# A fused attention and FFN block: the causal mask leaves the matrix engine, and the gate and up products are dealt over other beats

## The reference

```python
x = L0_attn_x                              # (4, 512, 512)
xn = _layernorm(x, axis=-1)
s = _L0_attn_ref(xn, w_qkv, w_out, q_gamma, k_gamma)
g = _silu(_L0_ffn_ref(xn, wq_gate, s_gate, wq_up, s_up, wq_down, s_down))
x = x + s * g

# attention: 16 heads of 32, per-head rmsnorm of q and k, rope, causal
mask = (q_idx >= k_idx) & (q_idx - k_idx <= WINDOW)      # WINDOW 1024 > 512
scores = einsum('bhqd,bhkd->bhqk', q, k) / sqrt(HD)
attn = softmax(where(mask, scores, NEG))
out = einsum('bhqk,bhkd->bhqd', attn, v) ... @ w_out

# ffn: W = (wq - 128) * scale, hidden size 1408
qlinear(silu(qlinear(x, wq_gate)) * qlinear(x, wq_up), wq_down)
```

## Time and profile before

| what | value |
|---|---|
| median of 3 runs | 791.72 us (791.6 to 792.12) |
| time of the profiled execution | 793.75 us |
| its span | 791.8 us |
| PE, PE weight load busy | 716.0 us, 575.5 us |
| DVE, ACT, POOL busy | 530.2, 450.1, 293.0 us |
| granted PE clock, mean of the span | 0.963 |

### The profile page before, as it was taken

One profiled execution on the slowest core, in us unless ns is written; L12 is line 12 of the kernel. 1 busy time (PEld: TensorE's weight loads), 2 busy tenths in 40 slices (PEclk: granted clock), 3 DMA queues, 4 the chain that ended last, 5 costly groups with the idle time before them and its releaser, 6 DMA issues.

```text
span 791.8 us, 12942 instructions
## 1 busy us (share of the span) xinstructions
PE 716.0 (90%) x4160; PEld 575.5 (73%) x4160; DVE 530.2 (67%) x1051; ACT 450.1 (57%) x1007; POOL 293.0 (37%) x338
## 2 busy tenths in 40 slices
PE   2589999989999999899999999999999944898997
PEld 2568887777787887777878777788887733676885
DVE  2677778887767676877666778777645673546373
ACT  1445666677666556776665567756555754534230
POOL 5443335555343344554443536544434310100000
PEclk9699999999999999999999999999999985699999
DMA  8154443412232332133333331233322163288672
GB/s 280 42 174 149 146 134 119 136 54 80 89 113 89 115 107 80 42 90 91 111 94 100 107 95 34 50 99 107 100 87 78 55 206 128 84 262 293 199 252 94
DMA packets 59281, 94.38 MB, mean 119 GB/s; under 512 B 12752, under 2 KB 15440, under 8 KB 59216
## 3 DMA queue, kind: packets, MB, share of 16 engines
q1 hardware_dynamic: 59216, 93.56, 37.4%
HBM read 59.06 MB, written 25.82 MB: 107 GB/s over the span
## 4 chain that ended last, share of the span: by engine, by line
PE 68%; DMA 7%; issue 7%; DVE 6%; POOL 6%; SPq 4%; ACT 2%; DVEq 0%; POOLq 0%; ACTq 0%
PE bank L1124 18%; PE bank L1019 14%; PE bank L1060 7%; PE bank L1140 6%; PE bank L1100 6%; PE bank L1081 5%; PE bank L1044 4%; PE bank L1031 3%; POOL rr L517 2%; PE bank L1046 2%; DMA rd_dram<-rd 2%; PE bank L1083 2%; POOL rb L526 2%; DMA rdb<-rd_dram 1%; SPq L346 1%
## 5 line engine op out<-in xcount | busy, mean ns | idle before, releaser
L517 POOL TENSOR_TENSOR rr<-ss,half 128x8 f32<-128x8 f32 x64 | 106.1, 1658 | 161.8 <-DVE ss L791 161.8
L842 DVE TENSOR_REDUCE mx<-bank 128x1 f32<-128x384 f32 (+3 forms) x176 | 109.6, 637 | 83.9 <-PE bank L1083 83.1
L625 ACT ACTIVATE pf<-bank 128x512 f32<-128x512 f32 (+1 forms) x192 | 100.7, 525 | 103.7 <-PE bank L1046 69.7
L823 DVE TENSOR_TENSOR pl<-pf,ph 128x512 fp32r<-128x512 f32 (+1 forms) x192 | 124.6, 649 | 19.0 <-ACT ph L626 18.8
L1124 PE MATMUL bank<-xnt_h,wgu 128*128 128x512 f32 x352 | 98.7, 402 | 4.6 <-DVE g L869 2.0
L523 POOL TENSOR_TENSOR ra<-qn,cg 128x256 f32<-128x256 f32 x64 | 58.2, 909 | 118.5 <-DVE qn L803 118.5
L626 ACT ACTIVATE ph<-bank 128x512 fp32r<-128x512 f32 (+1 forms) x192 | 100.9, 525 | 0.0
L1044 PE MATMUL bank<-qst,kst 97*128 97x512 f32 (+3 forms) x256 | 83.0, 377 | 16.1 <-DMA qst<-mrow 16.1
L1124 PE MATMUL bank<-xnt_l,wgu 128*128 128x512 f32 x352 | 96.3, 395 | 0.0
L1081 PE MATMUL bank<-kst,qst 96*128 96x128 f32 (+3 forms) x256 | 83.5, 377 | 1.3 <-DVE mx L842 1.3
L1060 PE MATMUL bank<-ph,va 128*65 128x512 f32 (+3 forms) x256 | 77.7, 328 | 5.0 <-ACT oraw L634 3.1
(11 more groups left out here) (84 smaller groups left out, 1406.8 us busy)
## 6 DMA issues: line engine op xcount, KB each, us to landing
wgu<-wg_dram SPq DMA_DIRECT2D x66, 256.0 KB, 2.8
hf_dram<-g SPq DMA_DIRECT2D x44, 256.0 KB, 3.2
hf_raw<-hf_dram SPq DMA_DIRECT2D x44, 256.0 KB, 5.8
wg_dram<-wgu SPq DMA_DIRECT2D x22, 256.0 KB, 3.1
xr<-x SPq DMA_DIRECT2D x16, 256.0 KB, 3.6
stage<-w_gu SPq DMA_DIRECT2D x16, 256.0 KB, 3.3
oh<-oraw SPq DMA_DIRECT2D x64, 64.0 KB, 2.0
ol<-oraw SPq DMA_DIRECT2D x64, 64.0 KB, 2.0
```

The lines of the kernel that those rows point to most:

```text
L517: pool.tensor_tensor(rr[:, s, :], ss[:, s, :], half[:], ALU.pow).then_inc(rr_ok, 1)
L625: act.activation(pf[:, tile], bank[:, 0:w], ACT.Exp, scale=SCALE)
L823: dve.tensor_tensor(pl[:, tile], pf[:, tile], ph[:, tile].bitcast(F32), ALU.subtract).then_inc(pl_ok, 1)
L842: dve.tensor_reduce(mx[:].rearrange("p (h t) -> p h t", t=TB)[:, h0:h0 + len(heads), qb], bank[:, 0:len(heads) * w].rearrange("p (h n) -> ...
```

## The change

- **No mask matmuls.** `scores_t` and `maxima` issue the score matmuls alone. For the maxima DVE now runs one `tensor_tensor_reduce` per head (it adds `msk_w`, a bf16 mask of 512 columns that is zero but for its last 128, writes the sum back to the bank and gives the maximum); in the compiled kernel each is an ISA instruction and a second one that writes the 128 x 1 result. There are 256 pairs in place of 160 reductions over scores. For the probabilities POOL zeroes what lies above the diagonal by `affine_select` on the high and low part together (`keep_past`, 128 x 2 x 128, 4 per head, 256 in all), and `p_v` waits for it (`tri_ok`). `norm` moves from k = 2 to k = 3.
- **Two beats of transposes.** The 4 row blocks of the next batch are transposed two by two in the places 9 and 10; the second of a beat goes through the bank of the gate products.
- **Gate and up products** of the batches 1 to 3 are dealt over 14 beats, from place 11 on: 1, then eight times 2 (places 12 to 3), then 1 in the places 4 to 8. Batch 0: two in each of the beats -3 to 6, one in 7 and 8.

```diff
-FIRST, PER_BEAT = -3, (2, 2, 2, 2, 2, 2, 2, 2, 1, 2, 1, 2)
+FIRST = (-3, -5, -5, -5)
+PER_BEAT = ((2, 2, 2, 2, 2, 2, 2, 2, 2, 2, 1, 1),) + ((1, 2, 2, 2, 2, 2, 2, 2, 2, 1, 1, 1, 1, 1),) * 3
...
+        def xt_at(c):
+            if c < 0:
+                return [(0, c + 7)] if 0 <= c + 7 < TB else []
+            b, k = c // 16 + 1, c % 16 - 9
+            return [(b, 2 * k), (b, 2 * k + 1)] if k in (0, 1) and b < B else []
+        def xt_bank(b, t):
+            return GU_PS if b and t % 2 else W_PS
...
+            def keep_past(j, e):
+                pool.wait_ge(pl_ok, NOP * j + e + 1)
+                for _, c0, _ in ST_OPS[e]:
+                    a = ST_AT[e] + c0
+                    op = pool.affine_select(pp[:, :, a:a + P], pp[:, :, a:a + P], [[0, 2], [1, P]], ALU.is_ge, 0.0,
+                                            base=0, channel_multiplier=-1)
+                op.then_inc(tri_ok, 1)
...
                 if there(j + 6, NB):
                     inv_rms(j + 6, (c + 6) % 2)
+                if there(j, NB):
+                    keep_past(j, 0)
                 if there(j + 6, NB):
                     rope(j + 6, (c + 6) % 2, (c + 6) % 4)
+                if there(j, NB):
+                    keep_past(j, 1)
...
-                if k == 2 and there(4 * r + (c - 6) // 4, B * G):
-                    norm(4 * r + (c - 6) // 4)
+                if k == 3 and there(4 * r + (c - 7) // 4, B * G):
+                    norm(4 * r + (c - 7) // 4)
+                if there(j, NB):
+                    keep_past(j, 2)
...
-                    dve.tensor_reduce(mx[...][:, h0:h0 + len(heads), qb],
-                                      bank[...], AX.X, ALU.max).then_inc(sm_ok, 1)
+                    for a, h in enumerate(heads):
+                        col = h * TB + qb
+                        op = dve.tensor_tensor_reduce(
+                            bank[:, a * w:(a + 1) * w], bank[:, a * w:(a + 1) * w], msk_w[:, N - w:N], 1.0, -3.0e38,
+                            ALU.add, ALU.max, mx[:, col:col + 1])
+                    op.then_inc(sm_ok, 1)
...
-                    pe.matmul(bank[:, c0:c0 + w], kst[...], qst[...], start=True, stop=False)
-                    op = pe.matmul(bank[:, c0:c0 + P], idb[:], msk_t[:], start=False, stop=True)
+                    op = pe.matmul(bank[:, c0:c0 + w], kst[...], qst[...], start=True, stop=True)
...
-                pe.wait_ge(pl_ok, NOP * j_ + e + 1)
+                pe.wait_ge(tri_ok, NOP * j_ + e + 1)
```

More of the change, by code:

```diff
@@ L222, in halves @@
         def halves(c):
[L224 to L228, removed]
+            for b in range(B):
+                rel = c - 16 * b - FIRST[b]
+                if 0 <= rel < len(PER_BEAT[b]):
+                    first = HALVES * b + sum(PER_BEAT[b][:rel])
+                    return list(range(first, first + PER_BEAT[b][rel]))
+            return []
         def half_at(c, index):
@@ L692, in o_out, with xn_out @@
                         o_evac(j - 1, 4 * r + (c - 1) // 4, (c - 1) % 4)
-                def xn_out():
-                    d, t = at(c, 9)
-                    if t is not None and there(r + 1 + d, B):
-                        xt_high(r + 1 + d, t)
+                def xn_out(index):
+                    for b, t in xt_at(c)[index:index + 1]:
+                        xt_high(b, t)
                 if turned:
                     t_high(j + 5, (c + 5) % 2)
-                xn_out()
+                xn_out(0)
                 gate(half_at(c - 1, 1))
@@ L903, in beat @@
                 gated(half_at(c - 1, 1))
-                d, t = at(c, 9)
-                if k != 3 and t is not None and there(r + 1 + d, B):
-                    xt_low(r + 1 + d, t)
+                if k != 3:
+                    for b, t in xt_at(c)[:1]:
+                        xt_low(b, t)
                 if mxs:
                     maxima(r, c + 4, SM_A[k])
-                if k == 3 and t is not None and there(r + 1 + d, B):
-                    xt_low(r + 1 + d, t)
+                if k == 3:
+                    for b, t in xt_at(c):
+                        xt_low(b, t)
                 if rms and k == 3:
@@ L1161, in turn_q @@
                             pe.wait_ge(s_ev, 4 * (r + d_o) + t_o + 1)
-                        if t_x is not None and there(r + 1 + d_x, B):
-                            pe.wait_ge(xt_lo, 4 * (r + 1 + d_x) + t_x + 1)
+                        for b, t in xts[:1]:
+                            pe.wait_ge(xt_lo, 4 * b + t + 1)
                         turn(r, c + 5, 0)
@@ L1176, in w_bank @@
                         out_proj(r + d_o, t_o, part)
-                    if part == 0 and early and t_x is not None and there(r + 1 + d_x, B):
-                        xn_turn(j + 4, r + 1 + d_x, t_x)
+                    if part == 0 and early:
+                        for b, t in xts:
+                            xn_turn(j + 4, b, t)
                 def w_free():
@@ L1190, in beat @@
                     scores_t(r, c, 0)
-                if not early and t_x is not None and there(r + 1 + d_x, B):
+                if not early and xts:
                     w_free()
-                    xn_turn(j + 4, r + 1 + d_x, t_x)
+                    for b, t in xts:
+                        xn_turn(j + 4, b, t)
                 if attend:
@@ L1212, in beat @@
                 turn_q()
-                if t_o is None and t_x is None:
+                if t_o is None and not xts:
                     banks(SM_B)
```

66 lines of the change are left out of this document (33 added, 33 removed).

## The result

The changed kernel takes 749.24 us (median of 4, 747.23 to 753.24) against 791.92 (median of 4 beside it): the ratio is 0.9465, 95% interval 0.9425 to 0.9506. The profiled execution took 753.24 us, the slowest of the four and 4.0 above their median, with a span of 751.2.

The account below looks back on a forecast made before the run. PE was taken to bound the middle, the `qn` loop the light beats. Savings of 6.5, 9.5, 9.5, 11.5, 1.0 and 1.5 us made 39.5: 754.3 for the profiled execution, 752 us against the median, range 740 to 760.

Parts of the forecast that it names:

- The likeliest case: Whole kernel: the forecast itself, a time of 740 to 760 us, chance 0.46.
- the `qn` loop: QKV bank's way from ACT to DVE, POOL and back to DVE, 7 to 8 us; the second limit, holding places 8 to 11.
- DVE's 90%: Sign against the forecast: DVE busy over 90% of a beat.
- The PE term: PE's work a batch: 128 masks at 0.125 us go, 16.0 us less, from 153.16 to 137.2.
- The stall terms: PE stalls a batch: 0.4 us in each of 12 full beats, 4.8, and 5.0 idle in the light beats.
- The DVE term: Masked reductions on DVE: 0.6 us a beat on top of 7.1, so 7.7 against PE's 8.6.
- The POOL term: Four selections a beat on POOL at 0.6 us each: from 4.5 to 6.9 us a beat.
- the second rival: DVE or POOL binds mildly, as selections slow DVE operations with two SBUF inputs: 760 to 782 us, chance 0.26.
- Beats 48 to 56: Late stretch with three gate products fewer: 85.1 us for 95.84, counted as 11.5 saved.
- beats 0 to 15: First batch with three gate products more: 141.2 us, 6.5 saved of 147.72.
- The ends: Before beat 0, 1.0 us saved; from 628.63 us on, 1.5 saved.
- The shadow rival: The 0.085 us delay might belong to score matmuls, not masks: 43 us of gain go, about 790; chance 0.03.

Follow-up runs that it names:

- e3: Changed kernel with the mask matmuls of `scores_t` put back and no selection on POOL: 771.71 us, ratio 0.9746 to the kernel before.
- e5: Changed kernel without POOL's selection and nothing in its place, so the value product lacks the causal mask: 756.14 us (one run).
- e4: Changed kernel with the mask matmuls of `maxima` and the plain reductions put back: 761.61 us, ratio 0.9619 to the kernel before.
- e6: Changed kernel with plain reductions over the unmasked scores in place of the masked ones: 744.57 us, ratio 0.9425 to the kernel before.
- e11: e5 with one wait more, holding POOL's `out_sum` and `norm` until DVE's subtraction of e = 1 is done: 740.63 us (one run).
- e8: Changed kernel with 60 unread filler matmuls at beat 60, where PE waits for a DMA: 747.24 us, ratio 0.9444 to the kernel before.
- e2: Changed kernel with both kinds of mask matmuls and plain reductions back, no selection, new deal kept: 783.76 us, ratio 0.9901 to before.
- e9: Changed kernel with every POOL selection done twice, with a wait between the two: 779.81 us (one run).
- e1: Changed kernel with the old deal of gate products and transposes, masks still out of PE: 762.88 us, ratio 0.9646 to before.

## Why the prediction was right, and which terms were not

752 us was forecast and 749.24 measured. The likeliest case came, and what bounds the middle was read rightly: PE in the full beats, the `qn` loop in the light ones. That the number is so close is partly luck, as the terms behind it were missed in opposite directions. In the profiled execution the beats 0 to 56 saved 46.1 us where 37.0 were forecast, and the two ends lost 5.5 where 2.5 were to be won: 40.6 in all, for 39.5 in the sum. Of the signs that it named, place 6 (9.88 us), the start behind a 384-column score matmul (0.175) and the short waits on `qn` came about as said, places 3 and 15 took 9.93 and not at most 9.6, places 8 to 11 took 29.8 and not 32, and DVE's 90% was passed in the light beats.

- **The PE term** was 16.0 us a batch, 0.125 a mask. PE's busy time a batch fell by 12.8 (153.16 to 140.32), 0.10 a mask, so it is 140.3 and not 137.2. The price was read at a 384-column matmul, where it holds. The masks of `scores_t` give 0.11 each where PE is never idle (e3 against e5), those of `maxima` 0.07 beside 128 columns and 0.12 beside wider ones (e4 against e6), and nothing in places 8, 9 and 12, as the prediction said of the light beats.
- **The stall terms**, 4.8 us in full beats and 5.0 in light ones, were too large. PE idles 3.3 us a batch in all (143.67 - 140.35), as before: 2.1 in places 8 to 11 (29.80 - 27.70), 1.2 in the 12 others. The two misses, 3.1 too little PE work and 6.5 too much stall, leave the batch 3.3 under the forecast 147.0.
- **The DVE term** was right in kind and size: 0.70 and 0.14 us for the two instructions, 120.16 / 16 = 7.5 us a beat against 7.7. In the path the masked reductions cost 1.1 us a batch (e6).
- **The POOL term** was 0.6 us a selection; it is 0.44. Its price in the path is 1.66 us a batch, once the collision is held still (e11).
- **Contention**, the second rival, is real, but smaller than priced and with a second effect that it did not have. It put 1.2 us a beat of it on DVE; against e11 it is 0.35 (5.66 / 16). And the selections moved one collision away from an instruction that PE waits for, which was worth more than they cost (e5, e11). The rule of the Trainium skill in SBUF — State Buffer, Who interferes with whom, that a DVE instruction with two SBUF inputs contends with a GpSimd instruction that reads SBUF, fits them: the subtraction has both inputs in SBUF and POOL's sum reads two tiles there (0.69 to 1.54 us).
- **Beats 48 to 56** came out at 83.8 us for 85.1, beats 0 to 15 at 140.7 for 141.2.
- **The ends** were to save 2.5 us and cost 5.5 in the profiled execution, 3.4 by the medians (42.7 saved in all, 46.1 of them in the middle). The granted clock is lower there than before: from 37 us on the start ran at 1.00 before and at 0.86 now, and the end at 0.86 and 0.82. Part of that is this one execution: beat 0 starts at 73.3 us in it, but at 71.3 in e8 with the same code up to there, and at 70.4 in e6. But there is a pattern in the traces. Between 37 us and beat 0 the clock was at half for 0 to 1.1 us in the three kernels that have the mask matmuls of `maxima` (before, e2, e4), and for 0.2 to 10.5 us in the eleven that do not. That a PE with fewer matmuls in thin stretches gets the lower level more often was not in the prediction. It does not explain the later start by itself: e6 has 6.8 us at half there and reaches beat 0 first of all, e8 has 0.2 and is 0.8 behind it. What the clock costs at the start was not tried.
- **The shadow rival** held in part: the 128-column score matmuls stay 0.11 us apart without any mask, where two value products of 128 columns stay 0.05 apart before (377.40 to 377.45). Whether their weight loads, 128 columns for the scores and 65 for the values, are the reason was not tried. Its price was also added wrongly: 752 and 43 are 795, not about 790.

The two rows of the start, before and after, from the first full clock to beat 0:

```profile
36.75:70.74 33.99, 28.90 (x172) 23.95 (x170) 25.77 (x52) 16.09 (x35) 13.69 (x17) 1.00 0.41 133
```
```profile
37.20:73.30 36.10, 31.32 (x155) 26.91 (x154) 26.68 (x72) 16.02 (x36) 13.47 (x17) 0.86 0.38 125
```

Fewer matmuls (155 for 172) take longer, and a part of them runs at half clock.

## What to carry to other kernels

Price a small matmul by the distance between starts, and take that distance from neighbours of the same width: what a removed neighbour gives back depends on how close the ones left can get. When work moves to an engine that had idle time, look at what it pushes back on that engine, and which instruction elsewhere then runs beside it; a delay can be worth more than the work costs, and the same gain is had by one wait. When an experiment takes one thing out, compare it with a kernel that differs in that alone: e3 beside the changed kernel mixes the masks, the selections and the collision, e3 beside e5 does not. Work removed from beats that another loop holds buys little, and the time can even grow where the clock then falls, so even the beats out together with it.

## What the runs showed of the hardware

- A DVE subtraction with both inputs in SBUF takes 0.69 us for 512 columns alone and 1.54 when POOL's sum of two SBUF tiles (1.28 us) begins 0.30 us before it: its end lies 0.13 us ahead of where it would be if it began when POOL had ended. The order of two such instructions is worth 3.8 us a batch (e5, e11).
- A masked reduction from PSUM that writes its sum back takes 0.70 us for 512 columns and 0.32 for 128, plus a second instruction of 0.14 for the result.
- A selection over 128 x 256 in place takes 0.44 us on POOL in the mean and 0.41 in the median, about half of a product of two tiles of the same size (0.84 in the mean, `L533`).
- In e9 and e1 the granted clock fell to 0.5 (the 1.2 GHz level) in the middle of the kernel, behind beats with several short waits of PE; the longest single one ahead of the fall was 1.6 us in e9 and 1.3 in e1.
- Keeping PE busy through a wait of 15 us lifted the mean clock of the 29 us behind it from 0.50 to 0.71, and the four heads in it took 22.8 us for 23.3, as they then waited more for POOL's selection.
